# Correction products stored column by column and summed over a strided axis by one reduction a column

## What is computed

```python
L = H * W                                   # 1600 pixels, K = 17, PAD = 8
qkv = xt @ w_qkv.T + b_qkv
q, k, v = jnp.split(qkv, 3, axis=2)
q = (q * scale).reshape(B, L, HEADS, c1).transpose(0, 2, 1, 3)
def windows(t):
    img = jnp.pad(img, ((0, 0), (0, 0), (PAD, PAD), (PAD, PAD)))
    flat = _unfold(img, K)
    tw = flat.reshape(B, K2, C, L).transpose(0, 3, 1, 2)
    tw = tw.reshape(B, L, K2, HEADS, c1).transpose(0, 3, 1, 2, 4)
    return tw
attn = jnp.einsum('bhnc,bhnlc->bhnl', q, windows(k))
attn = jax.nn.softmax(attn, axis=-1)
attn = attn * mask_w[:, None]
out = jnp.einsum('bhnl,bhnlc->bhnc', attn, windows(v))
...
x = x + _L0_conv_ref(_ln_c(x), ...)         # attention and projection, then
t = t + _L0_ffn_ref(_ln_t(t), ...)          # the experts, on tokens
```

## Time and profile before

| | us |
|---|---|
| median of 3 runs | 502.24 |
| lowest, highest | 501.3, 503.28 |
| profiled execution | 503.64 |
| its span | 501.7 |

### The profile page before, as it was taken

How to read it: one execution, slowest core, us unless ns; L and a number is a source line. 1 busy time by engine, 2 the same in 40 slices (tenths; PEclk the granted TensorE clock), 3 DMA queues, 4 the chain that set the end, 5 groups by cost and what they waited for, 6 DMA issues and landing times.

```text
span 501.7 us, 16643 instructions
## 1 busy us (share of the span) xinstructions
PE 436.1 (87%) x6962; PEld 303.1 (60%) x6962; DVE 370.6 (74%) x903; ACT 256.3 (51%) x441; POOL 252.2 (50%) x270
## 2 busy tenths in 40 slices
PE   4999918798887878988789898898799999999996
PEld 2789915466665656766556666675655545766553
DVE  1241285899999999999999999994867652463553
ACT  2330067787787876887767676795000000252432
POOL 9401154897896969796969969590300000000110
PEclk9785569899999998999999999999689855879999
DMA  6079984877555654565545545459570000006500
GB/s 207 2 241 282 246 273 134 267 219 229 187 193 157 195 176 167 182 201 169 183 159 181 185 133 170 131 171 236 153 196 0 2 0 0 1 0 215 198 18 33
DMA packets 38904, 76.42 MB, mean 152 GB/s; under 512 B 9348, under 2 KB 25877, under 8 KB 38013
## 3 DMA queue, kind: packets, MB, share of 16 engines
q1 hardware_dynamic: 37966, 73.79, 47.2%
q0 software_dynamic: 144, 1.36, 0.8%
q10 hardware_dynamic: 720, 0.22, 0.2%
HBM read 44.94 MB, written 29.29 MB: 148 GB/s over the span
## 4 chain that ended last, share of the span: by engine, by line
PE 43%; DVE 36%; issue 13%; POOL 3%; DMA 2%; ACT 0%; SPq 0%; DVEq 0%; POOLq 0%; ACTq 0%
DVE slabs L1044 12%; PE ps L852 10%; DVE pm L1064 8%; DVE scn L1054 4%; PE ps L778 4%; PE ps L891 4%; PE ps L743 3%; PE ps L911 3%; DVE kprod L1014 3%; DVE ebd L1077 3%; PE ps L736 3%; DVE osel L1083 2%; PE ps L699 2%; PE ps L823 2%; DMA kimg<-qrot 1%
## 5 line engine op out<-in xcount | busy, mean ns | idle before, releaser
L778 PE MATMUL ps<-slabs 128*32 128x401 f32 x528 | 117.9, 514 | 15.4 <-POOL slabs L514 14.4
L778 PE MATMUL ps<-prb,slabs 128*32 128x401 f32 x494 | 113.8, 517 | 0.0
L653 ACT ACTIVATE exb<-scn,lowest 128x401 f32<-128x401 f32 x120 | 74.4, 622 | 26.3 <-DVE lowest L1054 25.7
L1044 DVE COPY_PREDICATED slabs<-con,zt 128x1152 f32<-128x1152 int32 x41 | 77.8, 1899 | 0.1
L562 POOL TENSOR_TENSOR xln<-xln,wide 128x400 f32<-128x400 f32 x4 | 4.9, 1229 | 136.2 <-DVE wide L1215 136.2
L783 PEld LDWEIGHTS ps<-con,slabs 128*32 128x32 f32 x960 | 41.9, 112 | 48.8 <-issue 48.5
L801 PE MATMUL ps<-con,exb 128*128 128x128 f32 x360 | 49.5, 282 | 24.4 <-DVE pm L1073 23.9
L1054 DVE CUSTOM_DVE_ANT_0 scn<-ps,con 128x401 f32<-128x401 f32 x120 | 63.0, 570 | 7.0 <-PE ps L783 7.0
L514 POOL TENSOR_TENSOR slabs<-con,sbd 128x384 f32<-128x384 f32 x40 | 50.4, 1262 | 31.5 <-DVE sbd L1029 31.5
L642 ACT ACTIVATE prb<-slabs 64x1169 f32<-64x1169 f32 x40 | 47.1, 1178 | 35.9 <-DVE slabs L1044 35.7
L531 POOL TENSOR_TENSOR kprod<-xln,wide 120x640 f32<-120x640 f32 (+1 forms) x36 | 58.6, 1628 | 9.7 <-DMA xln<-qd 9.7
(11 more groups left out here) (138 smaller groups left out, 766.3 us busy)
## 6 DMA issues: line engine op xcount, KB each, us to landing
slabs<-zsl SPq DMA_DIRECT2D x40, 539.5 KB, 3.7
zsl<-uv SPq DMA_DIRECT2D x44, 484.5 KB, 3.7
slabs<-combd SPq DMA_DIRECT2D x2, 1600.0 KB, 8.4
skb<-zsl SPq DMA_DIRECT2D x4, 539.5 KB, 7.3
slabs<-kimd SPq DMA_DIRECT2D x2, 881.7 KB, 12.4
vimd<-vimg SPq DMA_DIRECT2D x1, 1612.0 KB, 5.4
frd<-wide SPq DMA_DIRECT2D x2, 800.0 KB, 5.3
kimd<-prb SPq DMA_DIRECT2D x1, 1596.0 KB
```

Source lines behind the costliest of these rows:

```text
L653: nc.scalar.activation(v(ex[x & 1], a, (1, NC3)), v(scn, (x & 1) * NB * NC3 + a, (1, NC3)), ACT.Exp, scale=-1.0, bias=lowest[:, NB * (x & ...
L778: mm(bank(g, (1, NC3), parts=TW, p0=TW * i), w, v((kt, kh)[b & 1][x & 1], b // 2 * C, (1, NC3)), start=first, stop=False, skip_group_check ...
L1044: last = nc.vector.copy_predicated(v(kt[x & 1], 0, (C, NU), (1, C)), cv(name, (9, NU), (1, C), off=(1 - C - ph) % K).bitcast(I32), v(zt, a ...
```

## The change

The products of one column are now made and stored together: POOL's `boundary_mul(x)` multiplies 15 rows of 40 values, 600 elements, and stores them in 15 rows of 40 in one of two tiles. DVE's `boundary_add(x)` is one reduction that sums over the 15 rows, which it reads with a step of 40 values, and writes the 40 sums to `sbd`. `boundary(x)` waits for the sum of column x itself. The q rows are still loaded in chunks of 4 columns, but into one of two buffers: the old one and a new `qb2`, which POOL clears too. A chunk's products wait for all its 15 loads (one semaphore for each buffer). The two tiles of products lie in `xt`, and so SP loads the input image into `xt` once more, in its turn 38. In turn i POOL multiplies column i + 3 and DVE sums column i + 2; before the loop DVE multiplies columns 0 and 1 and POOL column 2. SP issues the group (i + 7) of q rows in turn i.

```diff
-        kprod, kacc = sb("kprod", NCC * XE), sb("kacc", 2 * XE)
+        qb.append(sb("qb2", NCC * XE))
+        kprod = [xt[:, i * NCC * SZ:(i + 1) * NCC * SZ] for i in range(2)]
...
             def q_load(c, g):
-                if c == 0:
-                    sp.wait_ge(S["qb_zero"], 1)
+                if c < 2:
+                    sp.wait_ge(S["qb_zero"], 2)
                     sp.wait_ge(S["qn_out"], 16)
                 else:
-                    sp.wait_ge(S["kmul"], 4 * (c - 1) + g + 1)
+                    sp.wait_ge(S["kmul"], XC * (c - 1))
...
-            for g in range(len(GROUPS)):
+            for g in range(len(GROUPS) - 1):
                 q_load(1, g)
             sp.wait_ge(S["v_copied"], NQ)
             images_out(sp, vimg, vimd, S["vim_out"])
             for i in range(SZ):
                 if i + 2 < SZ:
                     store(i + 2)
-                if i == 0:
-                    q_load(2, 0)
-                c, g = divmod(i + 9, XC)
+                c, g = divmod(i + 7, XC)
                 if c < NXC:
                     q_load(c, g)
                 if 2 <= i:
                     load(i)
+                if i == SZ - 2:
+                    sp.wait_ge(S["kadd"], SZ)
+                    for k in range(NQ):
+                        sp.dma_start(xt[:, k * Q:(k + 1) * Q], x_in[:, k * Q:(k + 1) * Q]).then_inc(S["x_in"], 16)
...
             def boundary(x):
-                pool.wait_ge(S["kadd"], x // XC + 1)
+                pool.wait_ge(S["kadd"], x + 1)
...
+            def boundary_mul(x):
+                c, xi = divmod(x, XC)
+                pool.wait_ge(q_in[c & 1], 16 * NCC * (c // 2 + 1))
+                pool.wait_ge(S["kadd"], x - 1)
                 n = 8 * NCC
...
+                gp.tensor_tensor(v(kprod[x & 1], 0, (SZ, NCC), (1, SZ), parts=n),
+                                 v(qb[c & 1], xi * SZ, (XE, NCC), (1, SZ), parts=n),
+                                 v(dkx, x * SZ, (SZ, NCC), (1, SZ), parts=n), ALU.mult).then_inc(S["kmul"], 1)
...
+            def boundary_add(x):
+
+
+                dve.wait_ge(S["kmul"], x + 1)
+                n = 8 * NCC
+                nc.vector.tensor_reduce(v(sbd, x * YP + 7, (1, SZ), parts=n), v(kprod[x & 1], 0, (1, SZ), (SZ, NCC), parts=n),
+                                        AX, ALU.add).then_inc(S["kadd"], 1)
...
-                if i == 0:
-                    boundary_add(1, 0)
-                c, g = divmod(i + 5, XC)
-                if c < NXC:
-                    boundary_add(c, g)
+                if i + 2 < SZ:
+                    boundary_add(i + 2)
```

More of the change, by code:

```diff
@@ L192, in program @@
         qn = frot
-        qb = xln
+        qb = [xln]
         qy = ebd
@@ L263, in program @@
         gk_in = [sem(f"gk_in{i}") for i in range(2)]
-        q_in = [sem(f"q_in{i}") for i in range(len(GROUPS))]
+        q_in = [sem(f"q_in{i}") for i in range(2)]
         weights_in = [sem(f"weights_in{k}") for k in range(1, NQ)]
@@ L500, in _ @@
             pool.wait_ge(S["qy_ready"], NQ)
-            gp.memset(qb[:], 0.0).then_inc(S["qb_zero"], 1)
+            for i in range(2):
+                gp.memset(qb[i][:], 0.0).then_inc(S["qb_zero"], 1)
             def spread(x):
@@ L542, in _ @@
             boundary(0)
+            boundary_mul(2)
             boundary(1)
[L544 to L545 removed]
             for i in range(SZ + 2):
@@ L551, in _ @@
                     mask(i)
-                c, g = divmod(i + 6, XC)
-                if (c, g) > (1, 1) and c < NXC:
-                    boundary_mul(c, g)
+                if i + 3 < SZ:
+                    boundary_mul(i + 3)
                 if i == SZ - 1:
```

53 lines of the change are left out of this document (10 added, 43 removed).

## The result

The changed kernel takes 522.95 us (median of 4 executions, 521.28 to 525.35) where the kernel before took 502.10 in the same comparison (4 executions). The ratio is 1.0418, with a 95% interval of 1.0378 to 1.0458: slower by 4.2%, and outside the predicted 496 to 510 us. The profiled execution took 521.28 us, with a span of 519.3 us against 501.7. The spans are 17.6 us apart and the medians 20.9: the profiled execution of the kernel before (503.64 us) was longer than any of its timed ones, and that of the changed kernel is its fastest.

A forecast was written before the change was run, and what follows sets the result against it. DVE's instruction list was taken to bound the column loop. Start -0.5, loop 0.0 and end of loop +1.8 sum to +1.3 us on the timed median of 502.24, giving 503.5 us, range 496 to 510.

The forecast's parts named there:

- What bounds the kernel: Column loop, iterations 4 to 33: DVE, busy 99%, sets the iteration with its list of instructions, 6.94 us before the change.
- The added wait and its order: Every iteration: `boundary` waits for its column's sum, DVE's copy queues behind POOL's product; iteration 6.80 us, loop gain 0.0.
- the short rows: POOL's product of 600 elements in rows of 40: 1.48 us forecast; rival that short rows pay, 508.5 us, 8%.
- the 0.07 us that it added on the columns from 27 up: Late loop iterations: 0.07 us added for five or six short instructions of `spread`, making 6.87 us.
- The reduction's price: DVE's new 600-element reduction per column: 0.69 us from start to start, its strided read taken as free.
- The size of the base: DVE's reduction without stride penalty: some 0.78 us long, from L1087 plus 480 elements at 1.02 ns each.
- strided read pays: Rival on DVE's reduction: 1.27 us each, 0.58 us more in each of 34 iterations, 523 us; 7%.
- The start: Before iteration 4: earlier scores of column 2, q loads behind the images; T4 at 107.7 against 108.24, -0.5 us.
- The end of the loop: From T34 to the scores of column 38: 22.7 us against 20.93, +1.8 us.
- The refill of `xt`: Four DMAs, 800 KB, on SP behind column 38's load: no cost, up to 2 us if the queue is slow.
- The rival "the copy goes first": DVE's copy precedes POOL's product: at each chunk's first column, 494.5 us, 8%; in every iteration, 481 us, 5%.
- The rival of the held end (L557 and `weigh`): Column 38: without the weighing's 4.82 us hold, column 39's products start about 2 us sooner; 501.5 us, 10%.

The follow-up runs named there:

- experiment 1: Changed kernel with the reduction reading its 15 values side by side (step 1), so wrong sums: 503.98 us, ratio 1.0022 to the kernel before.
- experiment 3: Changed kernel with single reductions, copies, sums and POOL products at various steps appended behind its end: profiled execution 554.21 us, appended work included.
- Experiment 9: Changed kernel with a second set of single instructions behind its end, steps in falling order and other offsets; no whole time given, step 2 costs 0.02 us at most.
- Experiment 7: Changed kernel with chunk 1's last three q loads ahead of the images and the `xt` refill behind the last slab's load: 515.95 us, ratio 1.0310 to before.
- experiment 5: Changed kernel with POOL storing products turned, reduction reading in a row, and POOL's product waiting for DVE's copy, first in its turn: 479.07 us, ratio 0.9575 to before.
- experiment 4: Changed kernel with POOL's product waiting for DVE's predicated copy and first in POOL's turn, strided read kept: 488.04 us, ratio 0.9726 to before.
- 8: Changed kernel with products stored turned and read in a row, product behind the copy, and q loads earlier with `xt` refill later: 473.11 us, ratio 0.9472 to before.
- experiment 6: Kernel before, with only POOL's product moved behind DVE's predicated copy and first in POOL's turn: 498.19 us, ratio 0.9953.

## Why the prediction was wrong, step by step

**What bounds the kernel: right.** DVE's list set the length of a turn before and after.

**The added wait and its order: right.** L518 is released by the reduction 36 times; a copy waits behind POOL's product in each of the turns 4 to 33 (30 of the 32 copies there; the second one of the two double turns doesn't wait); its median is 2.59 us where 2.5 was given. POOL's product takes 1.48 us, as was drawn from its longer and its shorter form, so the short rows cost nothing. With the read in a row (experiment 1) most turns are 6.76 to 6.82 us, where the sum gave 6.80, and the 30 turns take 207.20 us where it gave 208.1; the 0.07 us that it added on the columns from 27 up didn't come.

**The reduction's price: this is the step that failed.** The prediction put it at 0.69 us from start to start and measured is 1.24; 0.55 us in each of the 34 turns that DVE bounds are 18.7 us, and the time missed by 522.95 - 503.5 = 19.5. That these are so near each other is partly luck. By the marks of the two traces the loop missed by 15.7 us, the start by 2.4 and the two parts behind T34 together by -1.8, which is 16.3; the other 3.2 lie between the traces and the medians.

The size of the base came out right (0.758 us long in experiment 1, where 0.78 was given), but also by luck: it was taken from a copy at 1.02 ns an element, which was itself strided, and a reduction in a row happens to cost as much, (0.758 - 0.280) / 480 = 1.00 ns. By a copy in a row, at 0.63 ns, the same sum would have given an estimate of 0.58 us.

The error is in the reading of the two rows between which the price was bounded. The copy L985 was taken as a witness that a strided read is free, because its 1.02 ns an element looked like a price with no penalty in it. But nothing in the trace said what a copy in a row costs, and it costs 0.63 (experiment 3). The row had to be compared with its own unstrided form, and that form isn't in the trace of before; so it could bear out neither end. The other witness, L981, did have something to be compared with (L1054 in the earlier trace rows, another operation on PSUM with about as many elements, written in a row), gave 1.27 us, and came within 0.03 of 1.24 (0.41 us on 400 elements are 0.62 on 600, where the sum took 0.58; by the row itself it is 1.31). It was set aside because it strides its write and not its read. Experiment 3 shows that a strided write costs a copy even more than a strided read (1.14 against 0.73 us), so as a number L981's agreement is partly luck. But it had a comparison in it, and the trace of the kernel before has a second pair with one, which wasn't looked at: sums and products of two tensors in SBUF, first with both read in rows of 40 (L1002), then with one read at a step of 3 values and the other a single value for each row (L1137), by form as in the earlier trace rows:

```profile
L1002 DVE TENSOR_TENSOR wide<-slabs 120x1320 f32<-120x1320 f32 x1 | 1.5, 1521 | 0.0
L1137 DVE TENSOR_TENSOR zt<-rt,con 128x920 f32<-128x920 f32 x1 | 1.4, 1368 | 0.0
L1002 DVE TENSOR_TENSOR wide<-scn 120x840 f32<-120x840 f32 x1 | 1.0, 1025 | 0.0
...
L1137 DVE TENSOR_TENSOR zt<-rt,con 128x600 f32<-128x600 f32 x1 | 0.9, 940 | 0.0
```

From 840 to 1,320 elements the row reads go by 1.03 ns an element, from 600 to 920 the reads with step 3 by 1.34. Experiment 9 has the step of 3 alone in such a sum: 0.98 us on 600 elements, against 0.76 in a row.

The rival "strided read pays" had the mechanism and the time, 523 us, and was given 7%. Since the row against it had no comparison, nothing in the trace made it less likely than the forecast by such a margin; and an end of 20 us, about four times the forecast's other errors added up (1.5 + 1.7 + 2), belonged inside the range.

The Trainium skill ("SBUF — State Buffer", section "Door 1: The DMA port swizzle") has the rule that was held against the trace and lost. It says that full bandwidth needs two hits in a 16-byte line, and that each access which crosses to a new line pays. The runs agree with that: two values in a line (step 2) are free, one in a line (step 4 and more) pays, step 3 lies between. Where the same note puts the free limit at four fp32 values, the runs differ: a step of four already pays, 1.21 us against 0.77. The skill's page "VectorE: DVE Perf Modes", section "The perf-mode tier table (the rule you actually need)", lists a copy of fp32 in SBUF as twice as fast as an operation of the base mode, and the reduction at the base mode alone. The runs agree in kind (0.38 us against 0.69 from start to start, in a row), so one can't be priced from the other.

**The start: direction wrong, 2.4 us.** T4 was put at 107.7 and came at 110.17. The working named the right resource: the last q loads of chunk 1 behind the images. But it landed them at 94.3 where the product could begin at 95.89 only, and PE's scores of column 3 followed at 99.73, not 98.2, at 0.85 to 0.88 us each where later ones take 0.50. Experiment 7 measures what the place in the queue is worth, with what it does to the clock: 5.4 us, nearly twice what I then expected of undoing it. In the kernel before those loads weren't needed so early; the change both brought their use forward and moved them back.

**The end of the loop: right.** +1.8 us were given for T34 to the scores of column 38. In the trace it is 357.55 - 333.92 = 23.63 us in place of 20.93, of which the reduction's excess in three turns is 3 x 0.48 = 1.4; with the read in a row (experiment 1) it is 22.55, where 22.7 was given. The refill of `xt` was put at nothing, with up to 2 us if the queue is slow. Experiment 7 bears this out for the part as a whole, not for the refill by itself.

**The rival "the copy goes first".** It didn't happen by itself, but its price was well judged: 481 us were given for it, and with the read in a row experiment 5 has 479.07, with DVE at 5.7 us a turn and PE at 6.2 late in the loop, as was worked out.

**The rival of the held end (L557 and `weigh`).** In the changed kernel the last instruction of the weighing is at most 264 ns long, so the hold of 4.82 us in the earlier trace rows is gone. But the part from T34 on didn't become shorter, and in experiment 7, where the hold is back with 4.39 us, it takes 48.42 us against 48.34. So no gain of 2 us shows; without the hold the last products waited for their slab. The hold is back in experiments 4, 5 and 8 too (3.65, 4.00 and 4.90 us), and that part takes 48.4 to 48.7 us there.

## What to carry to other kernels

Before an unusual access is priced from a row of another operation, look whether the trace has the same operation without it; a duration alone doesn't tell whether a price is already in it. If a sum must run over a strided axis, let the engine that has slack write the values turned, so that the engine that bounds reads them in a row: here POOL did it for 0.01 us and saved DVE 0.55. And when two engines exclude each other, the order in which their long instructions are asked for can be worth more than the instructions: place the long one of the engine with slack where the other works on operations with one input in SBUF.

## What was not expected of the hardware

- A step is free up to two fp32 values in DVE's reductions, copies and sums of two tensors, costs a little under half at three, and nearly all from four on. At a step of 40 that is 0.52 us more on 600 elements of a reduction or a sum (1.21 less 0.69, from start to start), at four 0.43 on a reduction; on a copy it is 0.26 at 40 (0.64 less 0.38). A step of 40 takes 0.08 to 0.09 us more than one of 39 or 41, and steps of 16, 32 and 64 take 0.06 less. What sets these small differences isn't shown.
- A strided write costs a copy on DVE 0.62 us on 600 elements from start to start (543.01 - 542.01, less 0.38), more than a strided read; on POOL it costs a product nothing (1.45 and 1.46 us). Strided reads do cost POOL: 1.48 us with one input at step 2, 1.74 at step 4 and at step 40, 2.59 with both inputs at step 40.
- The exclusion of the two engines isn't between any two instructions but between kinds. Beside POOL's product the weighing, with one input in SBUF and one in PSUM, is no longer than alone (experiment 4: a median of 0.547 us in the 68 instructions of 384 elements a partition that run beside it, 0.548 in the 10 that run beside nothing). Beside `boundary` the small reduction of `pick_sum` takes 278 to 283 ns in the changed kernel, and beside `spread` the large one takes 1.310 us at the median in experiment 4; the one of its 40 that runs 1.11 us beside a product takes 1.281. Against `boundary` it isn't tested, since `boundary` waits for it. The predicated copy and the group sums, with two inputs in SBUF, went from 1.44 to 2.6 and from 0.48 to 0.90 us. The Trainium skill ("SBUF — State Buffer", section "Who interferes with whom") says this of a DVE instruction with two SBUF inputs against a GpSimd instruction that reads SBUF; the runs agree, experiment 6 most plainly, where the hold left one such instruction and took up the next.
